# Gathered node rows as three bf16 parts instead of f32 operands in a graph network kernel

## The reference, cut to what matters

```
rows = table[src]
msg  = rows * weight[:, None]
out  = segment_sum(msg, dst, n)
```

## Time and profile before

| what | us |
|---|---|
| median of 3 timed executions | 9433.94 (9428.69 to 9439.14) |
| span of the profiled execution | 11044.3 |
| POOL busy in the span | 5820.6 (53%) |
| PE busy | 4003.0 (36%) |
| DVE busy | 3958.5 (36%) |
| ACT busy | 1410.5 (13%) |

### The profile page before, as it was taken

One profiled execution on the slowest core, in us unless ns is written; L12 is line 12 of the kernel. 1 busy time (PEld: TensorE's weight loads), 2 busy tenths in 40 slices (PEclk: granted clock), 3 DMA queues, 4 the chain that ended last, 5 costly groups with the idle time before them and its releaser, 6 DMA issues. The chain is left out here.

```text
span 11044.3 us, 116200 instructions
## 1 busy us (share of the span) xinstructions
PE 4003.0 (36%) x18072; PEld 3408.2 (31%) x18073; DVE 3958.5 (36%) x9685; ACT 1410.5 (13%) x3057; POOL 5820.6 (53%) x5941
## 2 busy tenths in 40 slices
PE   1333423333345554321033443333333333333332
PEld 1333323333335552010033333333323333233332
DVE  5335664444445557920011111111122222422224
ACT  1000011111124445710000000000000000000000
POOL 0667744555430003777766666666645565356664
PEclk6555556666665555555556665555555555555555
DMA  1111103333332221000011111111111111111111
GB/s 42 43 42 42 44 25 92 93 90 91 89 88 81 81 81 36 1 21 21 7 54 52 53 53 47 42 42 43 43 39 40 41 42 42 35 41 42 42 43 41
DMA packets 364720, 548.58 MB, mean 50 GB/s; under 512 B 124102, under 2 KB 217114, under 8 KB 364650
## 3 DMA queue, kind: packets, MB, share of 16 engines
q0 software_dynamic: 186368, 330.08, 11.1%
q1 hardware_dynamic: 148330, 190.56, 5.6%
q10 hardware_dynamic: 29952, 27.28, 1.0%
HBM read 448.36 MB, written 99.13 MB: 50 GB/s over the span
## 5 line engine op out<-in xcount | busy, mean ns | idle before, releaser
L658 PE MATMUL PS<-GATHERED,OH 128*128 128x128 f32 (+1 forms) x10240 | 2403.2, 416 | 4359.3 <-issue 1547.1
L658 PEld LDWEIGHTS PS<-GATHERED,OH 128*128 128x128 f32 x10240 | 2145.9, 312 | 4664.6 <-issue 2130.2
L550 POOL DMA_INDIRECT GATHERED<-row_tab,IDX x2496 | 2464.6, 987 | 1899.6 <-issue 1030.8
L550 POOL DMA_INDIRECT GATHERED<-gat_tab,IDX x832 | 784.8, 943 | 898.4 <-DVEq L1505 509.8
L575 POOL DMA_INDIRECT list_dram<-REC_NOW,PLACE_NOW x832 | 912.5, 1097 | 313.8 <-issue 258.4
L550 POOL DMA_INDIRECT GATHERED<-typed_b_tab,IDX x832 | 817.9, 983 | 483.1 <-issue 241.0
L550 POOL DMA_INDIRECT GATHERED<-typed_tab,IDX x832 | 808.9, 972 | 479.6 <-issue 234.8
L715 PE MATMUL PS<-IDENT,GATHERED 128*128 128x128 f32 x3328 | 588.1, 355 | 968.6 <-DVEq L1505 823.1
L1220 DVE TENSOR_TENSOR X<-X,PS 128x128 f32 x512 | 146.6, 286 | 2013.7 <-remote 1305.8
L715 PEld LDWEIGHTS PS<-IDENT,GATHERED 128*128 128x128 f32 x3328 | 544.3, 188 | 1012.4 <-issue 1010.5
L1204 DVE TENSOR_SCALAR OH<-IOTA,DSTF,WF 128x128 f32 x2048 | 601.1, 361 | 678.5 <-issue 648.1
(11 more groups left out here) (243 smaller groups left out, 3912.5 us busy)
## 6 DMA issues: line engine op xcount, KB each, us to landing
gat_rows<-GATHERED SPq DMA_DIRECT2D x208, 264.0 KB
GATHERED<-gat_rows SPq DMA_DIRECT2D x208, 264.0 KB, 2.8
GATHERED<-row_tab,IDX POOLq DMA_INDIRECT x2496
ROWI<-dst_rows ACTq DMA_DIRECT2D x208, 128.0 KB
ROWI<-dst_rows SPq DMA_DIRECT2D x208, 128.0 KB
GATHERED<-gat_tab,IDX POOLq DMA_INDIRECT x832
list_dram<-REC_NOW,PLACE_NOW POOLq DMA_INDIRECT x832
GATHERED<-typed_tab,IDX POOLq DMA_INDIRECT x832
```

What stands on the lines that cost most here:

```text
L550: pool.indirect_dma_start(out=rows, out_offset=None, in_=table, in_offset=bass.IndirectOffsetOnAxis(ap=IDX[:, k:k + 1], axis=0),).then_inc ...
L658: last = mm(bank(p)[:, 0:r.shape[1]], onehot(p, t), r, start=(t == 0), stop=(t == CT - 1))
```

## The change

- In the walks `l0`, `l2`, `l2b`, `l3a` and `l3b` the gathered rows are split into three bf16 parts in a new buffer `PARTS` of two halves. ACT rounds the rows to the high part (`part_hi`). DVE subtracts it from the rows in place (`rest`). ACT rounds the remainder to the middle part (`part_mid`). DVE writes the last remainder as the low part (`low`), and this instruction now gives the row buffer free.
- PE multiplies a bf16 one-hot by each part: 12 bf16 products a visit in place of 4 in f32. It waits for `free`, that is for `low`, in place of the landing.
- In `l3a` and `l3b` the weight leaves the one-hot. DVE multiplies the gathered rows by it first (`weigh_rows`), and the one-hot is the single unweighted instruction.
- In `l0` the weights are split once ahead of the walk (`w_split`) and ACT copies three parts of them beside the rows.
- `gb` and `g1` keep their f32 work. After each read of the chunk table, in all walks, the two counts are clamped to zero or above by two register operations.
- Semaphores `idx`, `onehot` and `sums` are shared by the five walks, with counts that run on.

```diff
+        OHB = OH[:, :].bitcast(BF16)
+        PARTS = sb("PARTS", [P, 2 * CT * NP3 * SEC], BF16)
             def read(c, p=0, table=RANGES):
                 eng.load(regs[p], table[0:1, bass.ds(c * REGS, REGS)])
+                for k in range(2):
+                    eng.reg_alu(counts[p][k], regs[p][k], 0, ALU.max)
...
                 for t in range(CT):
-                    r = rows(t)
-                    last = mm(bank(p)[:, 0:r.shape[1]], onehot(p, t), r, start=(t == 0), stop=(t == CT - 1))
+                    for n, r in enumerate(rows(t)):
+                        last = mm(bank(p)[:, 0:r.shape[1]], onehot(p, t, 1, r.dtype == F32), r, start=(t == 0 and n == 0),
+                                  stop=(t == CT - 1 and n == len(rows(t)) - 1))
+            def split_rows(name):
+                return lambda i, u: hold(pe, walks[name].free, RING * i + (RING + 1 + u))
...
+                def chunk(i, u, last_):
+                    c = RING * i + u
+                    hold(act, wk.gathered[u], 16 * CT * (i + (wk.rounds * NIT + 1)))
+                    if not last_:
+                        next_indices(wk, column, i, u)
+                    hold(act, parts_free, c + (wk.splits * NCH + 1))
+                    if weighed:
+                        hold(act, row_weighed, c + ((wk.rounds - 1) * NCH + 1))
+                    nc.scalar.activation(parts_of(u)[:, 0, :, :], rows_of(u), ACT.Copy).then_inc(part_hi, 1)
...
+                    hold(act, part_rest, c + (wk.splits * NCH + 1))
+                    nc.scalar.activation(parts_of(u)[:, 1, :, :], rows_of(u), ACT.Copy).then_inc(part_mid, 1)
...
-                for t in range(CT):
-                    last = v.tensor_scalar(onehot(p, t), IOTA[:, bass.ds(b * P, P)], DSTF[:, bass.ds(c * CT + t, 1)],
-                                           weights[:, bass.ds(c * CT + t, 1)], ALU.is_equal, ALU.mult)
+                def weigh_rows(i, c, u):
+                    hold(dve, wk.gathered[u], 16 * CT * (i + (wk.rounds * NIT + 1)))
+                    v.tensor_tensor(rows_of(u), rows_of(u), per_edge(weights, c, D), ALU.mult).then_inc(row_weighed, 1)
+                def rest(c, u):
+                    hold(dve, part_hi, c + (wk.splits * NCH + 1))
+                    v.tensor_tensor(rows_of(u), rows_of(u), parts_of(u)[:, 0, :, :], ALU.subtract).then_inc(part_rest, 1)
+                def low(c, u):
+                    hold(dve, part_mid, c + (wk.splits * NCH + 1))
+                    v.tensor_tensor(parts_of(u)[:, 2, :, :], rows_of(u), parts_of(u)[:, 1, :, :],
+                                    ALU.subtract).then_inc(wk.free, 1)
...
-                            onehots(c + 1, block_values((u + 1) % sets)[2], 1 - p, weights, column).then_inc(wk.onehot, 1)
+                            if not exact:
+                                if weights is not None:
+                                    weigh_rows(i + (1 if u == RING - 1 else 0), c + 1, (u + 1) % RING)
+                                rest(c + 1, (u + 1) % RING)
+                            onehots(c + 1, block_values((u + 1) % sets)[2], 1 - p, column, exact).then_inc(wk.onehot, 1)
+                            if not exact:
+                                low(c + 1, (u + 1) % RING)
...
-                        dve.nop(nofuse=True).then_inc(wk.free, 1)
+                        if exact:
+                            dve.nop(nofuse=True).then_inc(wk.free, 1)
+                        else:
+                            dve.nop(nofuse=True).then_inc(parts_free, 1)
```

More of the change, by code:

```diff
@@ L240, in __init__ @@
                 self.more_added = sem(f"more_added_{n}")
[L242 to L246, removed]
+        walk_l0 = Walk("l0")
+        walks = {"l0": walk_l0, "g1": Walk("g1", adds=False), "ga": Walk("ga", gathers=False, adds=False),
+                 "gb": Walk("gb", gathers=False), "l2": Walk("l2", splits=1, like=walk_l0)}
+        walks["l3a"] = Walk("l3a", rounds=1, gathered=walks["l0"].gathered, splits=3, like=walk_l0)
+        walks["l3b"] = Walk("l3b", rounds=2, gathered=walks["l0"].gathered, splits=4, like=walk_l0)
+        walks["l2b"] = Walk("l2b", rounds=1, gathered=walks["l2"].gathered, splits=2, like=walk_l0)
+        part_hi, part_rest, part_mid, parts_free = (sem(f"part_{k}") for k in ("hi", "rest", "mid", "free"))
+        row_weighed = sem("row_weighed")
         row_in = [sem(f"row_in_{u}") for u in range(RING)]
@@ L840, in indices @@
                         for u in range(RING):
-                            hold(act, wk.gathered[u], 16 * CT * (j + (wk.rounds * NIT + start + 1)))
-                            next_indices(wk, column, j + start, u)
+                            chunk(j + start, u, False)
                             if beside:
@@ L845, in indices @@
                     start += n
+                for u in range(RING):
+                    chunk(NIT - 1, u, True)
             for req in requests["before_l0"]:
@@ L851, in _ @@
                 answer(*req)
-            wk = walks["l0"]
-            first_indices(wk, SRCF)
-            def weights_beside(i, last_):
-                for u in range(RING):
-                    c = RING * i + u
-                    hold(act, wk.gathered[u], 16 * CT * (i + 1))
-                    nc.scalar.activation(G3[:, u * CT:(u + 1) * CT, D], WF[:, bass.ds(c * CT, CT)],
-                                         ACT.Copy).then_inc(weight_kept, 1)
-                    if not last_:
-                        next_indices(wk, SRCF, i, u)
-            with act.Fori(0, NIT - 1) as i:
-                weights_beside(i, False)
-            weights_beside(NIT - 1, True)
+            act.wait_ge(w_split, 1)
+            indices("l0", weights=True)
             for req in requests["l0_sums"]:
@@ L1216, in aggregate @@
                 wk = walks[name]
+                exact = ahead is not None
                 def add(b, p):
@@ L1249, in aggregate @@
                     read(0, 0, table)
-                onehots(0, block_values(0)[2], 0, weights, column).then_inc(wk.onehot, 1)
+                if not exact:
+                    if weights is not None:
+                        weigh_rows(0, 0, 0)
+                    rest(0, 0)
+                onehots(0, block_values(0)[2], 0, column, exact).then_inc(wk.onehot, 1)
+                if not exact:
+                    low(0, 0)
                 start = 0
```

85 lines of the change are left out of this document (51 added, 34 removed).

## The result

| | median us | ratio to before, 95% interval |
|---|---|---|
| before | 9433.26 (9428.69 to 9439.14, 4 runs) | |
| changed | 9970.35 (9968.27 to 9974.37, 4 runs) | 1.0575 (1.0563 to 1.0588) |

A forecast was written before the change was run, and what follows sets the result against it. POOL, issuing gathers back to back, was taken to bound the kernel. Added costs of 115 (l0), 83 (l2), 83 (l2b), 200 (l3a), 200 (l3b) and 5 sum to 686 us, set onto 9433.94: 10,120, range 9,650 to 10,550.

The forecast's parts named there:

- TensorE bounds nothing: In the split walks, 12 bf16 products take 1.5 to 2.7 us beside a 5 us period; gain from TensorE: nothing.
- POOL issues back to back: In timed executions POOL issues gathers without release waits; the sum is made in changes of its period, set onto 9433.94.
- Two SBUF inputs on DVE hold a gather: A DVE instruction reading two SBUF tensors early in a gather delays it; 130 ns an instruction in l2b.
- Rival A: Added instructions don't lengthen gathers; only the chain costs, 146 us each l3 walk, 70 in l0: about 9,790. Chance 0.13.
- 0.20 us an instruction: Gather delay per added DVE instruction with two SBUF inputs, in the split walks; bounds 0.13 and 0.33.
- 176 us of port: In l3a and l3b, 880 DVE instructions with two SBUF inputs a walk, at 0.20 us each, lengthen POOL's gathers.
- 24 us of margin: In l3a and l3b, a 5.7 us chain nearly level with POOL's 5.84 raises the period to 5.95, 200 us a walk.
- a chain of 13.3 us a pair of chunks: In l0's second half DVE exceeds POOL's 2 x 6.2; 6.5 us a chunk, 73 us of l0's 115.
- The reading of the two times: Whole kernel: POOL's 1626.0 us of waits belong to the profiled execution, explaining 11044.3 against the timed 9433.9.
- The sign named for that reading: POOL's waits vanish and the span falls by over 1,000 us while the timed median does not.
- rival C: Waits also in timed executions, or 2.7 us products in the chain, five walks: 10,500 to 11,000. Chance 0.08.
- Rivals B and D: B, 0.10: early release by `low`, 9,350 to 9,400. D, 0.05: all hidden behind POOL, within 0.2%.

The follow-up runs named there:

- the pair that differs in one operand: Before with clamps plus two unused DVE instructions a chunk in l2, l2b, l3a, l3b: two SBUF inputs 9732.11 us; first input in PSUM 9444.82 us.
- The pair of idle instructions: Before with clamps plus two DVE instructions a chunk from two SBUF tensors, result unread, in l2, l2b, l3a, l3b: 9732.11 us, ratio 1.0324.
- the last four runs: Chip 13, ratios to before: one-tensor one-hots with scan's ones in PSUM 1.0106, also rank steps moved 1.0065; changed kernel, one-hot first 1.0883, one-tensor one-hots 1.0811.
- the eight before them: On chip 15: clamps 9442.48; two added instructions 9732.11, one input in PSUM 9444.82; changed kernel edits 9626.67, 9971.02, 9898.15; one-hots from one tensor 9358.58, rank in PSUM 9358.48.
- two variants of the changed kernel: Changed kernel with the one-hot ahead of `weigh_rows` and `rest`: 12,007.59 us, ratio 1.0883; with one-hots from one tensor: 11,922.63 us, ratio 1.0811.

## Why the prediction was right, and where it was off

The forecast was 10,120 (9,650 to 10,550), slower. Measured 9970.35, 537 us where the sum said 686. By its steps, the terms as POOL's busy time in gathers, of the changed kernel less that of the kernel with the clamps (l2's rows as an example, with the clamps and changed):

```profile
L554 POOL DMA_INDIRECT GATHERED<-typed_tab,IDX x832 | 809.1, 972 | 253.5 <-issue 234.3 <-DVEq L1246 18.9 <-ACT IDX L835 0.3
```
```profile
L549 POOL DMA_INDIRECT GATHERED<-typed_tab,IDX x832 | 890.4, 1070 | 253.6 <-issue 241.7 <-DVE PARTS L1238 11.9
```

| term | sum | measured |
|---|---|---|
| l2 | 83 | 890.4 - 809.1 = 81 |
| l2b | 83 | 911.1 - 821.0 = 90 |
| l3a | 200 | 917.1 - 787.0 = 130 |
| l3b | 200 | 916.3 - 788.3 = 128 |
| l0 | 115 | 955.4 - 882.6 = 73 |
| g1 | 0 | 0 |
| elsewhere | 5 | 9 for the clamps; 165.6 - 151.2 = 14 in the wait for gat_tab |

The rows add up to 525; the other 12 us lie in small changes of POOL's idle time that I have not placed.

- **TensorE bounds nothing: right.** In the changed kernel the products, cut to a third, changed nothing.
- **POOL issues back to back, and the sum is one of its periods: right.** In the trace of the kernel with the clamps POOL waits 134.7 us for DVE's release in five walks together, in pieces no longer than its usual gap. In g1, though, POOL was not "far ahead": the earlier trace rows have 777.85 us of POOL beside 702.58 of DVE.
- **Two SBUF inputs on DVE hold a gather: right,** and shown by the pair that differs in one operand. The Trainium skill (SBUF - State Buffer, "Who interferes with whom") says that a DVE instruction with two SBUF inputs contends with a GpSimd instruction that reads SBUF, and the runs agree: 1066.3 us of such DVE time cost 290 us, 1060.6 us with one input in PSUM cost 2. The inference of that section that tensor_tensor leaves descriptor generation alone gives the wrong answer for these gathers. A gather here also reads its indices from SBUF, and whether that reading or the making of descriptors is what waits, no run can tell. Rival A, for which the inference spoke, is out.
- **0.20 us an instruction: near, and no constant.** 416 added in l2b cost 0.22 each, 880 in l3a 0.15; over the four walks it is 0.17. The reason given for taking 0.20, that a second instruction in a row catches the same gather again, did not occur in the changed kernel. The pair of idle instructions, where it did, had 0.08 to 0.29. That l2 and l2b came out at 171 for 166 owes something to luck.
- **The term that was mis-sized is l3.** Two errors lay in one direction. 176 us of port were 130. And 24 us of margin, for a chain of 5.7 us a chunk level with POOL, were nothing: the chain fits into 5.3, as the kernel with `rest` and `low` from PSUM shows. I had added up 0.64 for further blocks in full, and hand-overs of 0.15 (the 0.16 behind them is in none of the earlier trace rows, nor is it a hand-over between engines: at 6865.17 in that trace DVE's add has it as plain "issue"), where `rest` begins 0.11 behind the copy that it waits for (8005.79 to 8005.90) and the one-hot lies beside ACT.
- **l0** was put at 115 for 73, with the same error: a chain of 13.3 us a pair of chunks that was to exceed POOL. The changed kernel has 402 gathers in the 615 us from 870 on, 12.2 us a pair, with 14.0 us of waits for `low`. In the kernel before, moving rank to PSUM showed that DVE is not far behind; in the changed one it was not tried. (The two "comparisons of 1025" are rank's product and sum; its comparison takes 0.72.)
- **The reading of the two times was wrong in its cause.** I took the 1610 us between span and median for waits that belong to a profiled execution. The sign named for that reading came true, since the span fell by 1074.5 us, and yet the reading is wrong: all later profiled executions agree with their timed ones within 0.6%, and in the last four runs the timed ones of before are as long as that first span. The waits come from where or when the kernel runs, not from profiling. The last four ran on chip 13 and the eight before them on chip 15; on which chip the two executions ahead of the prediction ran is not on record, so chip and occasion can't be told apart. The sum did not suffer, since it was set onto the median and the changed kernel was timed where before takes 9433. For the other case rival C was right that the waits can be in timed executions too: there two variants of the changed kernel lost 8 to 9% to before.
- **Rivals B and D** (faster, or hidden) needed gathers that are not touched. The early release by `low` could give almost nothing, since POOL did not wait for longer than its usual gap.

A better kernel came out of it for the chip on which POOL bounds: before with the clamps and the one-hots from one tensor, 9358.58 for 9433.69.

## What to carry to other kernels

When an engine of descriptor issue sets the pace, count what its neighbour reads, not how busy it is: each DVE instruction with two SBUF inputs can hold back an indirect gather that starts inside it, for the rest of its length (0.31 us on average for each of 431 gathers of l3a). Move one operand to PSUM, or use a scalar column, and check the gather's mean. Before splitting an f32 product for TensorE, leave out most of the products for one run; if the time stays, a faster product has nothing to win. And compare a profile's span with the timed median before you read its waits: where they differ by 17%, as here, the waits may be those of another chip or occasion.

## What the runs showed of the hardware

- A gather that begins inside a 128x512 DVE instruction with two SBUF inputs ends 0.81 to 0.87 us after it (431 of 449 in l3a of the changed kernel), where alone it takes 0.94. The end of two in a row decided in some cases (2.11 us, in the kernel with the two idle instructions) and the end of the first in others (all 547 of the changed kernel). A scan held one longer still, and with its ones in PSUM it held none. From the changed kernel's timeline in l0:

```profile
1000.56 1.95 DVE L1437 TENSOR_TENSOR_SCAN EX<-ONE,H,EX 128x832 f32<-128x832 f32 x1 [0.20 <-DVE EX L1390]
1000.89 2.38 POOL L549 DMA_INDIRECT GATHERED<-row_tab,IDX  x1 [0.30 <-issue]
```

- It cuts both ways. In l3a of the changed kernel a one-hot that began 0.02 us ahead of a gather left that at 0.94 and took 0.74 itself, where others take 0.68 to 0.69:

```profile
8001.93 0.74 DVE L1209 TENSOR_TENSOR OH<-IOTA,DSTF 128x512 bf16 x1
8001.95 0.94 POOL L549 DMA_INDIRECT GATHERED<-row_tab,IDX  x1 [0.30 <-issue]
```

- One and the same kernel on one core took 9,433 us on one chip and 11,032 on another; whether the chip or the occasion made the difference is not shown. Where it is slow, the gathers of g1 take the 943 ns that they take elsewhere, and DVE has up to 3252.9 us of waits whose end no row explains.
